# Nine routed expert tiles move in between the matmuls of the last two gather chunks, with own places for all tiles and SyncE closing the level loop

## The reference

```python
def _L1_gnn_ref(input, adj, M, W, b, a):        # graph layer
    h = jnp.tanh(input @ W + b)
    inp = input @ W
    e = (h @ a)[:, 0]
    ...
    w = jnp.where(mask, jnp.exp(scores - m), 0.0)
    att = w / jnp.maximum(denom, 1e-30)
    return att @ inp                            # the "gather"

def _L1_ffn_ref(x, Wg, bg, W1, b1, W2, b2):     # 8 experts, the best 2 of each node, summed
    _, idx = jax.lax.top_k(x @ Wg + bg, K)
    ...
    h = jax.nn.gelu(jnp.einsum('td,edh->teh', xf, W1) + b1[None], approximate=False)
    y = jnp.einsum('teh,ehd->ted', h, W2) + b2[None]
    out = jnp.einsum('ted,te->td', y, mf)
```

## Time and profile before

| what | us |
|---|---|
| median of 3 runs | 837.11 (836.39 to 837.85) |
| span of the profiled execution | 873.3 |
| gather's matmuls on PE, first to end of last (L1397) | 551.5 to about 691 |
| tail, first to last result scatter on POOL (L1647) | 709.3 to 850.1 |

### The profile page before, as it was taken

How to read it: one execution, slowest core, us unless ns; L and a number is a source line. 1 busy time by engine, 2 the same in 40 slices (tenths; PEclk the granted TensorE clock), 3 DMA queues, 4 the chain that set the end, 5 groups by cost and what they waited for, 6 DMA issues and landing times. The chain is left out here.

```text
span 873.3 us, 11391 instructions
## 1 busy us (share of the span) xinstructions
PE 723.2 (83%) x3372; PEld 424.4 (49%) x3372; DVE 571.8 (65%) x1658; ACT 491.2 (56%) x741; POOL 196.0 (22%) x233
## 2 busy tenths in 40 slices
PE   2758999999999999999929978799899785776740
PEld 1543444444444444444418966354445374665640
DVE  7785668788888878787864787556555662534325
ACT  1746888888888888888827785222312241222210
POOL 2240000000000000000005531015434456565560
PEclk9969999999999999999958997799999876889875
DMA  4108989899999989887530000401100122222208
GB/s 130 69 0 262 288 260 262 255 273 253 259 258 260 272 249 275 243 255 223 165 128 8 1 2 0 122 5 39 33 25 29 56 67 68 73 79 74 79 18 288
DMA packets 100893, 124.58 MB, mean 143 GB/s; under 512 B 9038, under 2 KB 78930, under 8 KB 100576
## 3 DMA queue, kind: packets, MB, share of 16 engines
q1 hardware_dynamic: 96288, 115.32, 45.9%
q0 software_dynamic: 4544, 8.54, 3.0%
HBM read 88.54 MB, written 36.20 MB: 143 GB/s over the span
## 5 line engine op out<-in xcount | busy, mean ns | idle before, releaser
L552 DVE SCALAR_TENSOR_TENSOR probs<-adj,probs 128x1024 f32<-128x1024 int32 x128 | 156.7, 1224 | 77.0 <-ACT probs L525 68.0
L475 PE MATMUL ps<-x,qT 128*128 128x512 f16 x768 | 188.0, 382 | 3.2 <-PEq L198 3.2
L525 ACT ACTIVATE probs<-ps 128x1024 f32<-128x1024 f32 x128 | 130.9, 1023 | 51.0 <-PE ps L475 51.0
L536 ACT ACTIVATE mask<-probs 128x1024 fp8e4<-128x1024 f32 x128 | 134.0, 1047 | 0.0
L487 PE MATMUL ps<-probs,v 128*128 128x512 f32 x256 | 130.8, 592 | 0.0
L1397 PE MATMUL ps<-mask,parts 128*128 128x512 fp8e4 x512 | 119.7, 391 | 8.1 <-DVE parts L1664 8.1
L475 PEld LDWEIGHTS ps<-x,qT 128*128 128x128 f16 x768 | 75.5, 98 | 94.7 <-issue 5.7
L1571 ACT ACTIVATE mask<-ps,mask 128x256 f32<-128x256 f32 x78 | 32.6, 471 | 101.3 <-PE ps L1482 46.7
L1647 POOL DMA_INDIRECT mixed_spill<-mask,xn x78 | 76.3, 978 | 57.0 <-DVE mask L1794 32.3
L558 DVE TENSOR_TENSOR p_lo<-probs,p_hi 128x512 f16<-128x512 f32 x128 | 87.6, 684 | 0.1
L1600 POOL DMA_INDIRECT sorted_rows_spill<-rows,slots x64 | 62.8, 982 | 99.5 <-issue 54.4
(11 more groups left out here) (289 smaller groups left out, 975.3 us busy)
## 6 DMA issues: line engine op xcount, KB each, us to landing
adj<-in_adj SPq DMA_DIRECT2D x128, 512.0 KB, 4.8
sorted_rows_spill<-blank SPq DMA_DIRECT2D x32, 528.0 KB, 6.7
sorted_rows_spill<-blank SPq DMA_DIRECT2D x26, 198.0 KB, 7.4
xn<-sorted_rows_spill SPq DMA_DIRECT2D x39, 132.0 KB
mask<-mixed_spill SPq DMA_DIRECT2D x8, 512.0 KB, 6.3
mask<-in_x SPq DMA_DIRECT2D x4, 512.0 KB, 5.8
feat_spill<-mask SPq DMA_DIRECT2D x8, 256.0 KB
x_feat<-in_x SPq DMA_DIRECT2D x8, 256.0 KB, 4.8
```

The lines of the kernel that those rows point to most:

```text
L475: ins = nc.tensor.matmul(out, qT[:, q_half, j], kT[:, c, k_half * GROUP:(k_half + 1) * GROUP], start=(n == 0), stop=(n == 2))
L525: nc.scalar.activation(probs[:, k % RING, :], ps[:, b:b + 2, :].rearrange("p b n -> p (b n)"), ACT.Exp, scale=1.0 / QK_SCALE ** 2).then_in ...
L536: nc.scalar.activation(mask[:, k * W:(k + 1) * W], probs[:, k % RING, :], ACT.Sign, saturate=False).then_inc(mask_kept, 1)
L552: nc.vector.scalar_tensor_tensor(out=probs[:, k % RING, :], in0=adj[:, k % LOADS, :], scalar=0.0, in1=probs[:, k % RING, :], op0=ALU.is_gt ...
```

## The change

- `FIRST` = 9 of the 39 tiles now run inside the level. Their rows are worked out when 4 chunks are counted (`assign_tiles`, in chunk 5), and 8 more (to `EARLY` = 17) when 6 are counted (in chunk 7). `assign_tiles` stands behind `measure` and ahead of `choose`, where `early_tiles` stood behind `choose`.
- 11 "hooks" hold the nine tiles: behind each of the 8 groups of chunk 6 and the first 3 of chunk 7. Hook i runs up(i - 1), down(i - 2), turn_rows(i) on PE; `keep_outputs(i - 2)`, `keep_tokens(i)` on DVE; the Gelu of tile i - 1 and the weight copy of tile i + 1 on ACT (for these tiles ACT copies the weights, and DVE doesn't). They have one PSUM buffer of each kind where the tail has two.
- `sorted_rows` and `y` have a place for each of the 39 tiles, in the memory of the mask; no tile waits for the results of another to land.
- POOL scatters results 0 to 4 ahead of the rows of chunk 5, and 5 to 8 ahead of those of chunk 6.
- SP runs the level loop too: it loads the rows of tiles 0 to 8 and 9 to 16 in it, closes it, and raises `level_open` the first time, behind its five weight loads. PE leaves the level only when the rows of tiles 9 to 16 are in.
- The tail has tiles 9 to 38; the scatter of the last chunk's rows stands ahead of the results of tile 11, and the rows of tiles 17 to 38 are loaded after it.

The diff, cut to its core. `half`, `down_out` and the like choose PSUM buffers.

```diff
-EARLY_CHUNKS = 6
-EARLY = -(-(2 * GROUP * EARLY_CHUNKS - E * (2 * P - 1)) // (2 * P))
+FIRST_CHUNKS, SECOND_CHUNKS = 4, 6
+
+
+def tiles_known_full(chunks):
+    return -(-(2 * GROUP * chunks - E * (2 * P - 1)) // (2 * P))
+
+
+FIRST = tiles_known_full(FIRST_CHUNKS)
+EARLY = tiles_known_full(SECOND_CHUNKS)
...
+        region = buf("region", [P, E])
...
-        ROW_BANK, TURN_BANK, SMALL_BANK = 4, 6, 7
+        ROW_BANK, TURN_BANK, SMALL_BANK = 4, 4, 5
...
-        level_done = {name: sem(f"level_done_{name}") for name in ("pe", "act", "dve")}
+        level_done = {name: sem(f"level_done_{name}") for name in ("pe", "act", "dve", "pool")}
...
-        y = room.take(LOADS, 2, D)
-        both = room.take(RING, 2, SUB, D)
-        sorted_rows = xn_room.take(LOADS, 2, ROW)
-        XT_BANK, UP_BANK, Y_BANK = 0, 2, 4
-        CHOOSE_AT, STAGE_AT, RANK_AT, SCATTER_AT, TABLE_AT = 0, 0, 1, 2, 8
+        sorted_rows = room.take(ROUTED_STEPS, 2, ROW)
+        y = room.take(ROUTED_STEPS, 2, D)
+        both = Carver(xn[:, :, :].rearrange("p t d -> p (t d)")).take(RING, 2, SUB, D)
+        CHOOSE_AT, STAGE_AT, RANK_AT, SCATTER_AT, TABLE_AT = FIRST, FIRST, FIRST + 1, FIRST + 2, FIRST + 4
...
+        def half(k):
+            return (k - FIRST) % 2 if rest(k) else 0
...
+        def tokens_out(k):
+            return ps[:, half(k) if rest(k) else 7, 0:2 * P]
+
+        def down_out(k):
+            return ps[:, 6 + half(k), 0:2 * D] if rest(k) else ps[:, 7, 2 * P:2 * P + 2 * D]
+
+        def up_out(k):
+            return ps[:, 2 + half(k) if rest(k) else 6, :]
+
+
+        STEP_HOOKS = [(LAST - 1, g) for g in range(GROUPS)] + [(LAST, g) for g in range(FIRST + 2 - GROUPS)]
+
+        def steps_at(c, *groups):
...
-                count_ = sp.value_load(sb["levels"][0:1, 0:1], min_val=1, max_val=MOST_LEVELS)
-                sp.wait_ge(early_table, count_)
-                sp.sem_inc(moved_on, 1)
-                sp.wait_ge(early_landed, count_)
-                sp.sem_inc(moved_on, 1)
-                for k in range(ROUTED_STEPS):
-                    u = k % LOADS
-                    if k == EARLY:
-
-                        for n in range(SLOTS):
-                            sp.wait_ge(scattered[n], landed_rows(count_ + 1, n))
-                            sp.sem_inc(moved_on, 1)
-                        sp.wait_ge(last_scattered, PER_CHUNK)
-                        sp.wait_ge(rest_table, 1)
+
+                def load_rows(k, landed, before):
                     start = sp.value_load(table[0:1, 1, k:k + 1], min_val=0, max_val=E * N + (ROUTED_STEPS - 1) * 2 * P)
-                    if k >= LOADS:
-
-                        sp.wait_ge(y_out[u], 32 * (k // LOADS))
-                    sp.dma_start(sorted_rows[:, u, :, :], io["sorted"][bass.ds(start, 2 * P), :].rearrange("(h p) n -> p h n", p=P))\
-                        .then_inc(rows_in[u], 16)
-                for u in range(LOADS):
-                    sp.wait_ge(y_out[u], 32 * len(range(u, ROUTED_STEPS, LOADS)))
+                    if before:
+
+                        sp.wait_ge(landed, 16 * before)
+                    sp.dma_start(sorted_rows[:, k, :, :], io["sorted"][bass.ds(start, 2 * P), :].rearrange("(h p) n -> p h n", p=P))\
+                        .then_inc(landed, 16)
+
+                def level_of(level):
+                    sp.wait_ge(level_open, level)
+                    sp.sem_inc(entered, 1)
+                    sp.wait_ge(first_table, 1)
+                    for n in range(SLOTS):
+                        sp.wait_ge(scattered[n], landed_rows(level, FIRST_CHUNKS, n))
+                        sp.sem_inc(entered, 1)
+                    for k in range(FIRST):
+                        load_rows(k, rows_in[0][k % LOADS], k // LOADS)
+                    sp.wait_ge(second_table, 1)
+                    for n in range(SLOTS):
+                        sp.wait_ge(scattered[n], landed_rows(level, SECOND_CHUNKS, n))
+                        sp.sem_inc(entered, 1)
+                    for k in range(FIRST, EARLY):
+                        load_rows(k, rows_in[0][k % LOADS], k // LOADS)
+
+                    for n in range(SLOTS):
+                        sp.wait_ge(scattered[n], landed_rows(level, LAST, n))
+                        sp.sem_inc(entered, 1)
+                    for u in range(OUTS[0]):
+                        sp.wait_ge(y_out[0][u], level * (32 * len(range(u, FIRST, OUTS[0]))))
+                        sp.sem_inc(entered, 1)
+                    for done in level_done.values():
+                        sp.wait_ge(done, level)
+                        sp.sem_inc(level_closed, 1)
+                    for spent in each_level:
+                        sp.sem_clear(spent)
+                    sp.sem_inc(level_open, 1)
+
+                sp.sem_inc(level_open, 1)
+                levels(sp, level_of)
+
+                sp.wait_ge(last_scattered, PER_CHUNK)
+                sp.wait_ge(rest_table, 1)
+                for k in range(EARLY, ROUTED_STEPS):
+                    load_rows(k, rows_in[1][(k - EARLY) % LOADS], (k - EARLY) // LOADS)
+                for u in range(OUTS[1]):
+                    sp.wait_ge(y_out[1][u], 32 * len(range(u, ROUTED_STEPS - FIRST, OUTS[1])))
...
+                def step_of(i):
+
+                    if 0 <= i - 1 < FIRST:
+                        up(i - 1)
+                    if 0 <= i - 2 < FIRST:
+                        down(i - 2)
+                    if i < FIRST:
+                        turn_rows(i)
...
                             if c and g == 1:
+                                if c > 1:
+
+                                    pe.wait_ge(xT_ready, c - 1)
+                                    pe.wait_ge(ranks_read, c - 1)
                                 turn_sums(c - 1)
                             if c and g == 3:
                                 pe.wait_ge(rows_added, c)
-                                if c > 1:
-
-                                    pe.wait_ge(xT_ready, c - 1)
                                 turn(c - 1).then_inc(turned, 1)
                             if c and g == 4:
                                 pe.wait_ge(xT_ready, c)
-                                if c > 1:
-
-                                    pe.wait_ge(ranks_read, c - 1)
                                 gate().then_inc(gates_ready, 1)
                             if c and g == (6 if c == LAST else 7):
                                 pe.wait_ge(chosen_ready, c)
-                                (rank_and_total if c == EARLY_CHUNKS else rank)(c - 1).then_inc(ranked, 1)
+                                (rank_and_total if c in (FIRST_CHUNKS, SECOND_CHUNKS) else rank)(c - 1).then_inc(ranked, 1)
+                            for i in steps_at(c, g):
+                                step_of(i)
...
+                    for k in range(FIRST, EARLY):
+                        pe.wait_ge(rows_in[0][k % LOADS], 16 * (k // LOADS + 1))
+                    pe.wait_ge(tokens_ready[0], FIRST)
+                    pe.wait_ge(y_ready[0], FIRST)
                     pe.sem_inc(level_done["pe"], 1)
...
+                def load_weights(k):
+                    e_ = act.value_load(table[0:1, 0, k:k + 1], min_val=0, max_val=E - 1)
+                    if k >= WEIGHTS:
+
+                        act.wait_ge(y_ready[0], k - WEIGHTS + 1)
+                        act.wait_ge(down_ready[0], k - WEIGHTS + 1)
+                    nc.scalar.activation(current[:, k % WEIGHTS, :], weights[:, bass.ds(e_, 1), :].rearrange("p a n -> p (a n)"), ACT.Copy)\
+                        .then_inc(current_ready[0], 1)
+
+                def step_of(i):
+
+                    if i == 0:
+                        act.wait_ge(weights_in, 80)
+                        act.wait_ge(first_table, 1)
+                        load_weights(0)
+                    if 0 <= i - 1 < FIRST:
+                        gelus(i - 1)
+                    if i + 1 < FIRST:
+                        load_weights(i + 1)
...
                         scale_low_sums(c)
+                        steps(c + 1, 0, 1, 2)
                         if c == LAST:
                             break
                         act.wait_ge(turned, c + 1)
@@ -1551,31 +1671,25 @@
 
                             act.wait_ge(gates_ready, c)
                         keep_turned().then_inc(xT_ready, 1)
+                        steps(c + 1, 3, 4)
                         act.wait_ge(measured, c + 1)
                         if c >= SLOTS:
 
-                            act.wait_ge(scattered[c % SLOTS], landed_rows(level, c))
+                            act.wait_ge(scattered[c % SLOTS], landed_rows(level, c, c % SLOTS))
                         stage(c, 0).then_inc(staged, 1)
+                        steps(c + 1, 5)
                         stage(c, 1).then_inc(staged_again, 1)
+                        steps(c + 1, 6, 7)
...
-                pool.sem_inc(level_open, 1)
...
+                    for c in range(LAST - 2):
```

(62 more changed lines are left out.)

258 lines of the change are left out of this document (124 added, 134 removed).

## The result

The changed kernel takes 845.54 us (median of 4 runs, 844.76 to 846.06), the kernel before 836.75 in the runs beside it. The ratio is 1.0112, with a 95% interval of 1.0093 to 1.0131: the change costs about 9 us. Forecast were 843.0, within 833 to 850.

The account below looks back on a forecast made before the run. The prediction took the tail as bound by POOL (GpSimd), the gather by PE. Terms of 7.5 + 1.05 + 1.2 + 13.2 + 5.9 = 28.85 us more and 22.95 less gave 5.9 slower, 843.0 us, range 833 to 850.

Parts of the forecast that it names:

- The tail, -22.95: Tail: nine tiles leave GpSimd's row, 18 DMAs or 9 x 2.55 us, so 22.95 us less.
- the first profile's 28.5 us: Tail: GpSimd's idle time in the profiled run of the kernel before, taken as absent from a run without a profile.
- a register check of up to 1288 ns: Tail: SP's check, 18 ns in the median, read as a sign that the recording held the engines.
- the profiled pace: Rival, tail: a tile is worth 3.32 us and the nine 29.9, so the change is faster, 834.4 us; chance 0.25.
- the 36 us: Whole kernel: profiled span over median, 36.2 us, 28.5 of it put in the tail; counted against the faster case.
- The late opening and the table load, 7.5 + 1.05: Level's start: SP raises `level_open` behind five loads, 7.5 us later; ACT's new table load for `Exp` adds 1.05.
- The table in chunk 5, +1.2: Chunk 5: `assign_tiles` delays `choose`, so PE waits at `rank`: 1.2 us, from 0.6 to 1.8.
- PE's tile work: Gather: transposes, ups and downs add 13.2 us in chunk 6 and 4.6 in chunk 7.
- That rival: Rival, chunks 6 and 7: the hooks stall, 1 us on each of 8, giving 851 us; chance 0.11.
- Chunk 7, +5.9: Chunk 7: turn_sums comes 4.85 us later, 4.6 of tile work within, or 7 if gates come sooner; taken as 5.9.
- Leaving the level, 0 with a bound of 3: Level's end: PE waits for the rows of tiles 9 to 16; taken as 0 us, 3 as upper bound.
- Own places: Tail: own places for rows and results remove SP's and DVE's waits for landings, which gives nothing.

Follow-up runs that it names:

- `before_again`: The kernel before, unchanged, profiled once more: span 834.9 us, one run of 836.78 us.
- the extra DMAs: The kernel before with 13 more indirect DMAs on GpSimd in the tail, writing results again to an unread scratch tensor: 853.33 us against 836.43.
- `tables_moved`: The changed kernel with both tables of tiles made ahead of `add_rows` of the same pass, not ahead of `choose`: 837.64 us, ratio 1.0015.
- `before_own_places`: The kernel before with a place for every tile's rows and results, the only part of the change put in: 836.33 us, ratio 1.0002.
- the kernel with both edits: The changed kernel with both tables made ahead of `add_rows` and `level_open` raised by SyncE ahead of its weight loads: 828.88 us, ratio 0.9920.

## Why the prediction came out right, point by point

The forecast was that of a tail bound by GpSimd, and the sum was 5.9; the traces show 7.4 and the runs 8.8 (9.4 by the ratio). Part of that nearness is luck: the terms missed by 3.2 us to one side (chunks 5 and 7, leaving the level) and by 2.0 to the other (the opening, the clock up to chunk 4, the tail).

- **The tail, -22.95: right, measured -23.4.** A DMA costs 1.30 from start to start (105.2 / 81), not 1.275, since some take 1.1 to 1.2. The changed kernel's tail keeps that pace (81.81 / 63), so the loads behind the last rows' scatter came in time. That a plain run has none of the first profile's 28.5 us holds: `before_again` has none of it, and the extra DMAs cost their full price. What a register check of up to 1288 ns tells decided the case, for by the profiled pace the change would have won. What I read wrongly there is the gather: I saw hardly a gap in it, and counted against the profiled pace that the 36 us would then have to lie in the regular stretches, where 10.8 of them did lie. What slowed that one execution stays open. The Trainium skill (NOTIFIC — the notification-queue block, section 7.1) says that the internal pipeline of the profiler's records holds its producers back. That would fit, but no run here shows it, nor why one of two profiles of the same kernel has it.
- **The late opening and the table load, 7.5 + 1.05: right, measured 7.7 together, 0.85 less than the sum of both.** 6.8 are the opening's (10.8 less 4.0) and 0.9 the table load's. SyncE is held most by the load of b2b (3.75), then by that of b1b (1.65), and by the other three together for 2.2. The runs give the opening 8.1 (put in) and 7.9 (taken out), about 1 us more than the trace. The start of the block lies at 549.04 to 549.96 in the three traces with a late opening and at 547.36 to 549.01 in the nine others; whether the late opening has part in that I can't tell. The Trainium skill's 2.66 us for a switch, a drain included (ScalarE: Activation LUTs, "What ACT_TABLE_LOAD costs"), doesn't show here: 1.28 for the load and the Exp 0.02 behind it, on a ScalarE that had been idle for 11.56.
- **The table in chunk 5, +1.2: mis-sized, measured 2.0** (the line's 2.2 less 0.2 for hook 0), of which 1.77 is the wait at `rank`. So it came out at my upper bound of 1.8 or a little above, for the reason that I had given for it: without recording the gates come sooner, and then the whole table stands in PE's way.
- **PE's tile work: right.** Up to turn_sums of chunk 6 the gather grows by 15.1, after it by 2.7 of work, together 17.8, and 13.2 + 4.6 is the same. Only the border was off: my 13.2 for chunk 6 ends before hook 0 of chunk 7. PE is busy for 31.10 of 31.10 us, so the hooks stall nowhere. That rival is out.
- **Chunk 7, +5.9 with 4.6 of work in it, so 1.3 of waiting: too small.** The stretch grows by 5.5 with 2.7 of work, so 2.8 of waiting and lower clock, and with all 4.6 of the work it is 7.4, above my upper bound of 7. In the first profile PE waited 2.48 for `rank` anyway, which my step took as cover for the new table; in the second profile it waits nothing there and 3.24 at turn_sums. The changed kernel waits 3.56 and 1.61, so 1.9 more. The other 0.9 is the part that I missed: behind the 3.56 us the eight matmuls take 2.76 in place of 1.89. `tables_moved` gives back 4.6 of the 5.5.
- **Leaving the level, 0 with a bound of 3: measured 0.9.** SyncE's eight loads start at 709.37 and the last is issued at 717.8, because the second table, which SyncE waits for, is ready only at 707.95, and PE's first transpose comes at 720.98, 3.2 behind the last issue. A load took 1.05 where I had estimated 1.2. My step ended at the issue and left the landing out. PE stands 3.37, but the stretch to the last rows' scatter grows by 0.9 only.
- **Own places: nothing, as said.** Shown by `before_own_places`.

The errors in chunks 5 and 7 have, but for the 0.9 of the clock, one origin. The durations of single instructions in the first profile were sound; its waits were not. So the terms made of durations (13.2 + 4.6, 22.95, 7.5) came out within 1 us, and the two that rest on waits were 0.8 and 1.5 us off, to the same side: a disturbed trace shows slack that a plain run doesn't have.

What the change was good for is seen when its two faults are mended. Nine tiles cost PE 17.8 us in the gather and save GpSimd 23.4, a margin of 5.6, and `early_tiles` gone from behind `choose` is worth another 1.4 (what it gave in the kernel before; in this one it wasn't measured by itself). That makes 7.0, and the kernel with both edits is 7.1 under the kernel before. The late opening cost 8, the place of the two tables 8 more.

## What to carry to other kernels

Compare the span of a profile with the kernel's own time before reading any wait in it: where it is 4% longer, as here, profile again; here its durations held and its idle times did not. When work is moved from a bound engine under another's cover, check each new signal on the way, not only the work: who raises it, and what that engine has issued just before. A small serial chain belongs where its engine waits for something that can't come sooner, and making PE wait cost the wait and, behind 3.2 to 3.6 us of it, a slower clock.

## What I hadn't expected of the hardware

- A DMA of b2b (a broadcast to 128 partitions) held SyncE for 3.29 to 5.17 us at its issue in the twelve traces, that of W1b for 0.38 in each.
- PE at 1.00, idle for 3.56 us, was granted 0.67 in the mean of the next 2.8 us and 0.50 after; idle for 1.6 us, it kept 1.00 over the next 1.2 us of work, and had 0.50 after another 1.7 us of idle time.
- Two profiles of one kernel differed by 38 us in span (873.3 and 834.9) while the medians of its runs lay between 835.8 and 837.1, and in the longer one a register check of SP took up to 1288 ns that took 18 in the other.
